# One layer of a graph network on one core: the low part of the hidden layer and the doubling of x in four pieces each

## The reference

```python
msgs = feat[src]
neigh = jax.ops.segment_sum(msgs, dst, num_segments=feat.shape[0])
rst = (1.0 + eps[0]) * feat + neigh
h = jnp.maximum(rst @ W1 + b1, 0.0)      # 512 -> 1024
h = h @ W2 + b2                          # 1024 -> 512
return h + feat
# and around it: x = _layernorm(x + that, axis=-1)
```

## Time and profile before

| | us |
|---|---|
| median of three runs | 1085.34 |
| the profiled execution | 1085.76 |
| its span | 1084.0 |
| TensorE (PE) busy | 957.1 |
| POOL busy | 788.0 |
| VectorE (DVE) busy | 365.5 |
| ScalarE (ACT) busy | 253.5 |

### The profile page before, as it was taken

The page is one execution under the profiler, slowest core; times in us unless marked ns, Lnnn a source line. Parts: engine busy times, 40 slices in busy tenths (PEclk is TensorE's granted clock), DMA queues, the critical chain, the costliest instruction groups (busy, mean ns, idle before and its releaser), DMA issues.

```text
span 1084.0 us, 17939 instructions
## 1 busy us (share of the span) xinstructions
PE 957.1 (88%) x6340; PEld 605.5 (56%) x6340; DVE 365.5 (34%) x938; ACT 253.5 (23%) x512; POOL 788.0 (73%) x819
## 2 busy tenths in 40 slices
PE   1469889899899899899889989989989989899887
PEld 1126547556556556556546647647647646547556
DVE  4543333333332333333332332332332333333332
ACT  1123212212212222222212212212212212212212
POOL 6777777777777777777777777777777777777720
PEclk9979999999899999999999989989999999999999
DMA  6887887887877887787887887887887887887830
GB/s 195 275 282 209 243 243 212 248 244 214 239 239 219 242 245 217 238 245 215 236 244 214 243 247 204 244 246 202 244 247 202 246 248 206 243 241 205 249 107 20
DMA packets 86803, 243.92 MB, mean 225 GB/s; under 512 B 18343, under 2 KB 21134, under 8 KB 86774
## 3 DMA queue, kind: packets, MB, share of 16 engines
q0 software_dynamic: 64544, 210.95, 66.5%
q1 hardware_dynamic: 22230, 32.58, 9.3%
HBM read 229.85 MB, written 13.62 MB: 225 GB/s over the span
## 4 chain that ended last, share of the span: by engine, by line
POOL 62%; issue 23%; PE 8%; DMA 4%; DVE 1%; SPq 1%; POOLq 1%; ACT 0%; DVEq 0%; ACTq 0%
POOL raw L453 62%; PE hp L1112 3%; PE y L1128 2%; PE acc L1147 2%; DMA raw<-in_x_dram,idx 2%; DMA pairs<-beyond 1%; DMA win<-in_dst_dram 1%; POOL shared L501 0%; DMA late<-in_L_gnn_W_dram 0%; POOLq L278 0%; PE tables L1037 0%; SPq L329 0%; POOLq L506 0%; SPq L340 0%; DVE moments L934 0%
## 5 line engine op out<-in xcount | busy, mean ns | idle before, releaser
L453 POOL DMA_INDIRECT raw<-in_x_dram,idx x800 | 775.2, 969 | 245.3 <-issue 243.1
L1147 PE MATMUL acc<-raw,onehot 128*32 128x512 f32 x2200 | 320.3, 640 | 82.4 <-DMA raw<-in_x_dram,idx 80.0
L1112 PE MATMUL hp<-rstT_hi,w_hi 128*128 128x250 f32 x800 | 232.7, 291 | 4.2 <-DVE rstT_lo L910 4.2
L1112 PE MATMUL hp<-rstT_lo,w_hi 128*128 128x250 f32 x800 | 228.8, 286 | 0.0
L1112 PE MATMUL hp<-rstT_hi,w_lo 128*128 128x250 f32 x800 | 228.3, 285 | 0.0
L915 DVE TENSOR_TENSOR hT_lo<-late,hT_hi 128x500 fp32r<-128x500 f32 x100 | 68.2, 682 | 332.5 <-ACT hT_hi L586 332.5
L581 ACT ACTIVATE late<-hp,b1c 128x250 f32<-128x250 f32 x200 | 82.9, 466 | 395.6 <-PE hp L1112 395.6
L1112 PEld LDWEIGHTS hp<-rstT_hi,w_hi 128*128 128x128 f32 x800 | 155.0, 194 | 25.3 <-ACT late L581 15.9
L1112 PEld LDWEIGHTS hp<-rstT_lo,w_hi 128*128 128x128 f32 x800 | 155.5, 194 | 20.1 <-issue 20.1
L1128 PE MATMUL y<-w_hi,hT_hi 128*125 128x512 f32 x400 | 162.6, 407 | 0.0
L1128 PE MATMUL y<-w_hi,hT_lo 128*125 128x512 f32 x400 | 160.5, 401 | 0.0
(11 more groups left out here) (110 smaller groups left out, 458.1 us busy)
## 6 DMA issues: line engine op xcount, KB each, us to landing
raw<-in_x_dram,idx POOLq DMA_INDIRECT x800, 3.8
xt<-in_x_dram SPq DMA_DIRECT2D x50, 224.0 KB
out_dram<-late SPq DMA_DIRECT2D x50, 224.0 KB
late<-in_L_gnn_W_dram SPq DMA_DIRECT2D x7, 512.0 KB, 7.3
xt<-in_x_dram SPq DMA_DIRECT2D x50, 26.0 KB
out_dram<-late SPq DMA_DIRECT2D x50, 26.0 KB
win<-pairs SPq DMA_DIRECT2D x51, 16.0 KB, 3.2
rst<-in_L_gnn_W_dram SPq DMA_DIRECT2D x1, 512.0 KB, 14.7
```

The lines of the kernel that those rows point to most:

```text
L453: pool.indirect_dma_start(out=raw[:, i, k, :], out_offset=None, in_=table[:, :], in_offset=bass.IndirectOffsetOnAxis(ap=idx[:, slot, k:k + ...
L1112: mm = pe.matmul(hp[jp % 2][:, jj, :], w1[a][:, c, j * P:(j + 1) * P], rstT[b][:, half, c, :], start=(c == 0 and term == 0), stop=(c == TC ...
L1147: return pe.matmul(acc[i][q * QN:(q + 1) * QN, :], hot, rows, start=((q, k) == of_q[0]), stop=((q, k) == of_q[-1]))
```

## The change

`h_lo` makes `hT_lo` in four instructions instead of one: for each of the two chunks of the pair, each of the two tiles' 125 columns. `double_x` makes its 512 columns in four instructions of 128. Each piece counts up its semaphore once, and so the three places that wait for `s_hlo` or `s_double` wait for four times the count.

```diff
+LO_PIECES = 4
...
-                        act.wait_ge(s_hlo, PAIRS * m + jp - 1)
+                        act.wait_ge(s_hlo, LO_PIECES * (PAIRS * m + jp - 1))
...
             def h_lo(m, jp):
                 dve.wait_ge(s_hhi, PAIRS * m + jp + 1)
-                dve.tensor_tensor(hT[1][:, 2 * jp:2 * jp + 2, :], hfull[:, jp % 2, :, :],
-                                  hT[0][:, 2 * jp:2 * jp + 2, :].bitcast(F32), ALU.subtract).then_inc(s_hlo, 1)
+                for jj in range(2):
+                    for i in range(2):
+                        j, cols = 2 * jp + jj, slice(i * TN, (i + 1) * TN)
+                        dve.tensor_tensor(hT[1][:, j, cols], hfull[:, jp % 2, jj, cols],
+                                          hT[0][:, j, cols].bitcast(F32), ALU.subtract).then_inc(s_hlo, 1)
...
-                dve.scalar_tensor_tensor(out=xt[0:TN, slot, :], in0=xt[0:TN, slot, :], scalar=2.0,
-                                         in1=b2b[0:TN, :], op0=ALU.mult, op1=ALU.add).then_inc(s_double, 1)
+                for c in range(TC):
+                    cols = slice(c * P, (c + 1) * P)
+                    dve.scalar_tensor_tensor(out=xt[0:TN, slot, cols], in0=xt[0:TN, slot, cols], scalar=2.0,
+                                             in1=b2b[0:TN, cols], op0=ALU.mult, op1=ALU.add).then_inc(s_double, 1)
...
             def residuals(F, f, slot, stores):
-                dve.wait_ge(s_double, F + 1)
+                dve.wait_ge(s_double, TC * (F + 1))
...
-                        pe.wait_ge(s_hlo, PAIRS * m + j // 2 + 1)
+                        pe.wait_ge(s_hlo, LO_PIECES * (PAIRS * m + j // 2 + 1))
```

## The result

The changed kernel took 1075.94 us (median; 1074.3 to 1078.64) where the kernel before, in the same comparison, took 1084.1. The ratio is 0.9927, with a 95% interval of 0.9908 to 0.9946, 7.9 us. Timed again twice, beside other kernels, the ratio was 0.9923 (0.9894 to 0.9953) and 0.9923 (0.9895 to 0.9950). Forecast were 1075.0 and a gain of 10.8 us: the time came nearer to its forecast than the gain did, since the forecast starts from an execution of 1085.76, 1.7 us above the median that the result is compared with.

The account below looks back on a forecast made before the run. POOL's gathers, one after another, were taken as the bound. Excess of 12.9 + 1.5 = 14.4 us goes, 3.6 come back, 10.8 saved: 1085.8 - 10.8 = 1075.0 us, range 1071 to 1083.

Parts of the forecast that it names:

- POOL is the bound and its time comes back in full.: Gathers on POOL follow one another every 1.25 us, so all 10.8 us saved there come off the run.
- A gather waits for a two-input instruction, from 0.035 ahead to the request 0.127 behind.: A VectorE instruction with two SBUF inputs, in flight at a gather's request, holds it; h_lo 12.9 us, doubling 1.5 us.
- The inference cited against it: Such a tensor_tensor does not stall descriptor generation, so pieces would give nothing: 1085.8 us; rival of another cause, chance 0.06.
- The pieces cost 3.6 us.: Gather delay still caused by the pieces of h_lo and the doubling: 3.6 us, between formula 3.8 and actual starts 3.1.
- even spread: VectorE starts spread evenly over the 1.25 us between gathers: 0.025 us a train of four, 3.8 us for 150 trains.
- VectorE's 31 us more lie beside other work.: Trains on VectorE last 0.21 us longer than whole instructions, about 31 us over all 150, and delay no path now.
- The 2.0 us of the one-hots stay.: Gather delay beside 22 one-hot quarters on VectorE, 2.0 us, was taken as unchanged.
- the 953 of the forecast: Sign of being right: gathers from 62 us to the last tiles have a mean near 953 ns instead of 968.
- can lose the rest of one piece at most: POOL gets in between VectorE pieces, so a piece of 0.287 us costs a gather between 0 and 0.125 us.
- A gather that stands through more than one piece: Sign of being wrong; the rival that POOL does not get in between pieces had 1103.2 us, chance 0.03.
- TensorE takes over.: Rival: TensorE binds for part of the run, in half of the groups, so half the gain is lost: 1080.4 us, chance 0.14.
- TensorE's wait for gathered rows falls by about as much as the span: Sign of being right: TensorE's wait for gathered rows, 74.4 us before, shrinks about as much as the span.

Follow-up runs that it names:

- The kernel with all three remedies: Against the kernel before: h_lo reading PSUM, the doubling in pieces and a wait between the one-hots; 1073.57 us, ratio 0.9888.
- the same kernel without the waits: Against the kernel before: h_lo reading PSUM and the doubling in four pieces; 1075.03 us, ratio 0.9876; timed again 1072.92 us, ratio 0.9880.

## Why the prediction was right, and where it was off

*POOL is the bound and its time comes back in full.* Right up to the last gather: the pauses are equal, 7.3 us are off the gathers, and the last one starts 8.5 earlier with the 1.2 us of the start-up. The 1.2 and the 1.4 behind the last gather are no part of the sum: that the span fell by 9.9, near the 10.8, is luck in this execution. By the ratio over all runs it is 7.9.

*A gather waits for a two-input instruction, from 0.035 ahead to the request 0.127 behind.* Right, and now shown by taking the second input away: 14.0 us by the rule, none found. Only the 0.035 is too strict: in the first profile of the changed kernel a piece of h_lo that began 0.019 ahead of the gather at 90.13 cost it 0.134, where the prediction had 0.125 as the most. The inference cited against it (the Trainium skill, SBUF — State Buffer, "Who interferes with whom"), that such a tensor_tensor does not stall descriptor generation, gave no change. The 12.9 us that h_lo's second input cost the gathers, and the ratio of 0.9919 without it, decide against it.

*The pieces cost 3.6 us.* 2.9, 2.8 and 3.4 in three profiles. The formula behind it, even spread, was lucky: for two pieces it gave 4.9 where 10.3 were found. In the changed kernel no gather beside a piece of h_lo or of the doubling took over 1.08 us, as forecast.

*VectorE's 31 us more lie beside other work.* Right: 29.5 us more, and no new wait.

*"The 2.0 us of the one-hots stay."* This is the term that was mis-sized: it came to 5.5 to 5.7. The 3.5 us more, with the 0.7 at the weight and 0.7 less for the pieces than forecast, lead from 10.8 to the 7.3 of the gathers; their mean is 958 ns, not the 953 of the forecast. Two things went into it. The phases moved, so that 35 gathers met a one-hot instead of 23. And the prediction's "can lose the rest of one piece at most", read from trains in which POOL got in, is not a law: six gathers in each profile of the changed kernel were passed over. "A gather that stands through more than one piece" was among the prediction's own signs of being wrong, and it came true at the one-hots. In the changed kernel a wait between the one-hots ends it: none in two profiles, against six in each of three without it. (The kernel with all three remedies has none either, but the same kernel without the waits has none and one in its two profiles.) That overlap is the cause is not shown. In every one of these gathers, in all runs, the delay ended with the one-hot of the shared rows, which the wait keeps apart as well; a wait in front of that one alone was not run. Why the second and third quarters, h_lo's pieces and the doubling's, which overlap with the piece ahead of them as well, never passed a gather over (50 meetings with h_lo's and the doubling's in the first profile), and why the kernels with h_lo whole, in two pieces or from PSUM had none or one such gather (h_lo alone in four pieces had seven), stays open.

*TensorE takes over.* For the gathers it did not: POOL's pauses are as before up to the last one, so the 7.3 us are POOL's own. But the sign that the prediction set, that TensorE's wait for gathered rows falls by about as much as the span, failed: it fell by 3.5 us of 9.9. TensorE's busy time fell by 6.7 (957.1 to 950.4) at a mean granted clock of 0.971 against 0.962; how much of the span that gave is not shown. And behind the last landing on the chain, 964.5 us in this profile, TensorE sets the end, so that what a gather gains there no longer counts. The end moved with the gathers only to within 2 us: in the three profiles of the changed kernel the last gather begins 8.5, 8.0 and 5.7 us earlier, and the span is 9.9, 9.9 and 7.2 shorter.

## What to carry to other kernels

When GpSimd issues the gathers and sets the pace, look at each long one for a VectorE instruction with two SBUF inputs that ends with it: the sum of what they are late by, read from one trace, is the most that can be gained there. Take the second input from PSUM where that is free, since here that ended the conflict; pieces only bound what one meeting costs, and beside the one-hots not even that. Don't price meetings by an even spread alone: phases lock, and each change moves the phase of everything else that can collide.

## What the runs showed that was not expected

A gather that has asked and waits is not always served when the instruction in flight ends: the one-hot of 0.32 us that started 0.08 ahead of that end went first, and the next of 0.22 after it, so the gather lost 0.55. A wait between the instructions ended that in the changed kernel. It is not free on VectorE: a train of four one-hots lasts 1.47 us instead of 1.09, which cost no time here. The same tile in the run with waits:

```profile
252.04 1.47 DVE L694 TENSOR_TENSOR onehot<-iota_row,place 128x160 f32<-128x160 f32 x4
253.66 0.22 DVE L710 TENSOR_TENSOR onehot_shared<-iota_row,place_shared 128x64 f32<-128x64 f32 x1
```
